# Two-layer transformer block, eight batches: the layer-A maxima moved one group of heads earlier, the V copies on two engines

## The reference, cut to what matters

```python
B, S, D = 8, 512, 128
def layer_A(x):                      # x is the normalised input
    Q = split_heads(x, 16)           # queries are x itself: 16 heads of width 8
    K = split_heads(x @ Wk + bk, 16)
    V = split_heads(x @ Wv + bv, 16)              # width 32
    attn = softmax(Q K^T + causal_mask)
    return x + gelu(attn @ V) @ Wf + bf
def layer_F(x):                      # 8 heads of width 64, 8 experts
    q, k = heads(x @ w_q), heads(x @ w_k)
    gates = sigmoid(x @ w_gate); sel = argmax(gates); gm = one_hot(sel) * gates
    values = einsum('bhne,ehdk,bnd->bhnk', gm, value_experts, x)
    out = softmax(causal(0.125 q k^T)) @ values
    return einsum('bhne,ehkd,bhnk->bhnd', gm, output_experts, out).sum(heads)
x = x + layer_A(layernorm(x)); x = x + layer_F(layernorm(x))
```

## Time and profile before

| | us |
|---|---|
| three runs, median (lowest to highest) | 1350.18 (1346.76 to 1360.11) |
| the profiled execution, own time | 1347.51 |
| its span, first to last instruction | 1345.8 |
| PE busy in the span | 1160.4 (86%) |
| ACT busy | 967.8 (72%) |
| DVE busy | 872.1 (65%) |

### The profile page before, as it was taken

The page is one execution under the profiler, slowest core; times in us unless marked ns, Lnnn a source line. Parts: engine busy times, 40 slices in busy tenths (PEclk is TensorE's granted clock), DMA queues, the critical chain, the costliest instruction groups (busy, mean ns, idle before and its releaser), DMA issues.

```text
span 1345.8 us, 19795 instructions
## 1 busy us (share of the span) xinstructions
PE 1160.4 (86%) x5720; PEld 634.3 (47%) x5720; DVE 872.1 (65%) x2725; ACT 967.8 (72%) x2671; POOL 306.1 (23%) x418
## 2 busy tenths in 40 slices
PE   2797898898888989899888989889898898989998
PEld 1126643366424754247433564336642475434653
DVE  4625757577574866758576585756758486764845
ACT  3894777948597686966779577795779767696660
POOL 1023311232102411133112231123220241112220
PEclk8567999999999999999999999999999999989999
DMA  6211240022300323003320124102240032300310
GB/s 184 65 66 33 51 123 20 4 64 67 109 2 4 80 79 81 2 11 72 105 55 2 45 50 112 37 4 64 59 114 4 4 80 77 83 2 3 72 48 24
DMA packets 43644, 72.71 MB, mean 54 GB/s; under 512 B 9664, under 2 KB 25408, under 8 KB 43216
## 3 DMA queue, kind: packets, MB, share of 16 engines
q1 hardware_dynamic: 38416, 54.67, 15.0%
q10 hardware_dynamic: 5120, 16.78, 4.8%
HBM read 45.34 MB, written 8.80 MB: 40 GB/s over the span
## 4 chain that ended last, share of the span: by engine, by line
PE 38%; ACT 27%; DVE 15%; issue 12%; DMA 5%; POOL 2%; SPq 2%; ACTq 0%; DVEq 0%; POOLq 0%
ACT masked L838 13%; ACT pt L895 9%; PE ps_m L624 7%; PE ps_o L615 6%; DVE masked L1153 4%; PE ps_exp L441 3%; PE ps_max L721 2%; DVE pt L1304 2%; PE ps_exp L531 2%; PE ps_m L441 2%; PE ps_exp L443 2%; DMA s2q<-mt_f 2%; PE ps_exp L442 2%; PE ps_m L443 2%; PE ps_m L442 2%
## 5 line engine op out<-in xcount | busy, mean ns | idle before, releaser
L1153 DVE CUSTOM_DVE_ANT_0 masked<-ps_max,mask 128x512 f32<-128x512 f32 (+3 forms) x768 | 353.5, 487 | 207.9 <-PE ps_max L529 100.0
L838 ACT ACTIVATE masked<-masked,low 128x512 f32<-128x512 f32 (+3 forms) x768 | 426.1, 558 | 65.5 <-DVE low L1153 62.2
L895 ACT ACTIVATE pt<-ps_exp 128x384 f32<-128x384 f32 (+1 forms) x480 | 247.7, 523 | 95.7 <-PE ps_exp L532 75.6
L1036 POOL TENSOR_SCALAR_AFFINE_SELECT pt<-pt 128x512 f32<-128x512 f32 (+2 forms) x192 | 133.3, 695 | 697.3 <-ACT pt L895 697.3
L624 PE MATMUL ps_m<-at,oe_sb 128*128 128x512 f32 x416 | 220.7, 620 | 5.6 <-DVE at L1204 3.5
L615 PE MATMUL ps_o<-pt,val 128*32 128x128 f32 (+6 forms) x1536 | 191.9, 476 | 12.1 <-POOL pt L1036 11.6
L529 PE MATMUL ps_max<-s2k,s1q 72*128 72x512 bf16 (+3 forms) x512 | 141.8, 326 | 34.4 <-DMA s2k<-onesb_d 21.9
L1204 DVE TENSOR_TENSOR at<-osb,hots 128x512 f32<-128x512 f32 x208 | 145.3, 705 | 15.5 <-PE ps_m L624 15.5
L838 ACT ACTIVATION_READ_ACCUMULATOR masked<-masked,low 128x1 f32 x768 | 149.7, 195 | 0.0
L529 PE MATMUL ps_exp<-s1q,s2k 75*128 75x384 bf16 (+3 forms) x384 | 104.9, 324 | 44.0 <-ACT pt L895 41.5
L531 PE MATMUL ps_exp<-s1q,s1k 128*128 128x256 f32 (+2 forms) x256 | 100.1, 402 | 19.9 <-DMA s2q<-mt_f 19.7
(11 more groups left out here) (170 smaller groups left out, 1919.0 us busy)
## 6 DMA issues: line engine op xcount, KB each, us to landing
hots<-hot_d ACTq DMA_DIRECT2D x64, 256.0 KB, 4.1
s1q<-parts_q SPq DMA_DIRECT2D x96, 96.0 KB
s2k<-parts_k SPq DMA_DIRECT2D x96, 96.0 KB
s1q<-pt SPq DMA_DIRECT2D x64, 128.0 KB, 2.3
s1k<-pt SPq DMA_DIRECT2D x64, 128.0 KB, 2.3
parts_q<-pt SPq DMA_DIRECT2D x24, 128.0 KB, 2.3
parts_k<-pt SPq DMA_DIRECT2D x24, 128.0 KB, 3.0
x_sb<-in_x SPq DMA_DIRECT2D x8, 256.0 KB, 2.8
```

The lines of the kernel that those rows point to most:

```text
L838: last = nc.scalar.activation(e, e, ACT.Exp, bias=low[:, g % 2, c:c + 1], scale=-1.0, accum_out=den[:, g % 2, c:c + 1])
L895: nc.scalar.activation(pt[:, (n % 2) * 4 + j, 0:c1 - c0], score_bank(k, u)[:, c0:c1], ACT.Exp).then_inc(exp_done[k].sem, 1)
L1036: nc.gpsimd.affine_select(out=v, in_=v, compare_op=ALU.is_ge, fill=0.0, base=0, pattern=[[0, HG[k]], [0, m], [1, P]], channel_multiplier=- ...
L1153: last = v.tensor_tensor_reduce(out=masked[:, u % JUNK, c0:c0 + w], in0=src[:, c0:c0 + w], in1=mask[:, S - w:S], scale=-1.0, scalar=POS, o ...
```

## The change

- `FIRST` has two max units beside each of F's units 12 to 23: group 0 at 12 to 17, group 1 at 18 to 23. `negate` and the transposition of group 0 move to F's units 21 (DVE) and 23 (PE).
- Pre holds group 2 (for the first batch, which has no F ahead of it, groups 0, 1 and 2).
- The 12 max units of group 3 stand beside A's units 2, 3, 5, 7, 9, 11, 13, 14, 16, 18, 20 and 22 (`LATE`).
- The keys' preparation moves two units later in F, to the units 3 to 6.
- ACT copies V's tiles 1 and 3, DVE tiles 0 and 2, with two semaphores `va` and `vb`.
- In `turn` one kept product comes ahead of the back projection, and one product each takes the next place.

```diff
-FIRST = {FIRST_AT + n: (n,) for n in range(STAGES * HG["A"])}
+A_UNITS = STAGES * HG["A"]
+FIRST = {FIRST_AT + n: (2 * n, 2 * n + 1) for n in range(A_UNITS)}
+LATE = {2 + 11 * n // 6: n for n in range(A_UNITS)}
+NEGATE_A, TRANSPOSE_A = 21, 23
+def pre_groups(a):
+    return (0, 1, 2) if a == 0 else (2,)
-PREP = {"q1": 0, "q2": 0, "K": 1, "k0": 1, "k_rest": 2, "k1": 3, "k2": 4}
+PREP = {"q1": 0, "q2": 0, "K": 3, "k0": 3, "k_rest": 4, "k1": 5, "k2": 6}
...
# PE, values_a and the first score units
-                    dst = free("A", "V", t, (va, a, t + 1))
+                    dst = free("A", "V", t, ((va, vb)[t % 2], a, t // 2 + 1))
-                    pe.wait_ge(va.sem, va.count(b, T))
+                    pe.wait_ge(va.sem, va.count(b, T // 2))
+                    pe.wait_ge(vb.sem, vb.count(b, T // 2))
# PE, attention_a
-                            if g + 2 < GROUPS:
-                                max_unit("A", a, g + 2, s * HG["A"] + j)
+                            if u in LATE:
+                                if LATE[u] == 0:
+                                    pe.wait_ge(restacked_a[3].sem, restacked_a[3].count(a, 16 * RESTACK["A"]))
+                                max_unit("A", a, 3, LATE[u])
# PE, attention_f
+                                for first in FIRST.get(u, ()):
+                                    g_a, m = divmod(first, A_UNITS)
+                                    if m == 0:
+                                        pe.wait_ge(restacked_a[g_a].sem, restacked_a[g_a].count(f + 1, 16 * RESTACK["A"]))
+                                    max_unit("A", f + 1, g_a, m)
+                                if u == TRANSPOSE_A:
+                                    maxima_transposed("A", f + 1, 0)
# PE, turn
+                if f >= 0:
+                    product(f, first + 1)
                 project_back(a, (0, 1, 2))
                 if f >= 0:
-                    product(f, first + 1)
+                    product(f, first + 2)
# ACT
+            def firsts(a, u):
+                for first in FIRST.get(u, ()):
+                    g, m = divmod(first, A_UNITS)
+                    denominators("A", a, g, m)
+                    if m == A_UNITS - 1:
+                        logs("A", a, g)
+            def values_a(a):
+                for t in range(1, T, 2):
+                    act.wait_ge(v_ready.sem, v_ready.count(a, t + 1))
+                    copy(val[:, t], ps_m[BANK[("A", "V", t)]][:]).then_inc(vb.sem, 1)
...
                 if k == "F":
                     sums(k, b, GROUPS - 1)
                     if b + 1 < B:
-                        for first in FIRST[NST * HG[k] - 1]:
-                            denominators("A", b + 1, 0, first)
-                        logs("A", b + 1, 0)
+                        firsts(b + 1, NST * HG[k] - 1)
+                        maxima("A", b + 1, 0)
# DVE
-                for t in range(T):
+                for t in range(0, T, 2):
                     dve.wait_ge(v_ready.sem, v_ready.count(a, t + 1))
                     v.tensor_copy(val[:, t], ps_m[BANK[("A", "V", t)]][:]).then_inc(va.sem, 1)
-                if a > 0:
-                    negate("A", a, 0)
+                                if u == NEGATE_A:
+                                    negate("A", f + 1, 0)
```

More of the change, by code:

```diff
@@ L263, in build @@
         parts_out = {n: sem(f"parts_out_{n}", 16 * PARTS) for n in "qk"}
[L264 removed]
+        v_ready, va, vb = sem("v_ready", T), sem("va", T // 2), sem("vb", T // 2)
         resid = sem("resid", 2)
@@ L642, in attention_a @@
                 n_units = STAGES * HG["A"]
-                for g in range(2):
-                    if g == 0 and a > 0:
-                        continue
+                for g in pre_groups(a):
                     pe.wait_ge(restacked_a[g].sem, restacked_a[g].count(a, 16 * RESTACK["A"]))
@@ L650, in attention_a @@
                             outputs(a - 1, "pre", n)
-                        if g == 1 and n == n_units // 2 - 1:
+                        if a == 0 and g == 1 and n == n_units // 2 - 1:
                             maxima_transposed("A", a, 0)
                 for g in range(GROUPS):
-                    if g + 2 < GROUPS:
-                        pe.wait_ge(restacked_a[g + 2].sem, restacked_a[g + 2].count(a, 16 * RESTACK["A"]))
                     pe.wait_ge(mrow["A"][g % 2].sem, mrow["A"][g % 2].count(a, 16 * MROWS["A"] * (g // 2 + 1)))
@@ L728, in turn @@
                 f, first = a - 1, T * E - TURN
+                if f >= 0:
+                    product(f, first + 1)
                 project_back(a, (0, 1, 2))
                 if f >= 0:
-                    product(f, first + 1)
+                    product(f, first + 2)
                 project_back(a, (3,))
                 if f >= 0:
-                    for u in range(first + 2, T * E - 2):
+                    for u in range(first + 3, T * E - 2):
                         product(f, u)
@@ L865, in attention @@
                 outs = b if k == "F" else b - 1
[L866 to L872, removed]
+                if k == "A":
+                    values_a(b)
+                for g in (0, 1) if k == "F" else pre_groups(b):
+                    for n in range(n_units):
+                        denominators(k, b, g, n)
+                        if g == 1 and n == (1 if k == "F" else n_units // 2 - 1):
+                            maxima(k, b, 0)
+                    logs(k, b, g)
                 if k == "F":
@@ L896, in attention @@
                                                  ACT.Exp).then_inc(exp_done[k].sem, 1)
-                            if m > 0 and g + 2 < GROUPS:
+                            if k == "A":
+                                if u - 1 in LATE:
+                                    denominators("A", b, 3, LATE[u - 1])
+                                    if LATE[u - 1] == A_UNITS - 1:
+                                        logs("A", b, 3)
+                            elif m > 0 and g + 2 < GROUPS:
                                 denominators(k, b, g + 2, m - 1)
@@ L902, in attention @@
                             if k == "F" and b + 1 < B:
-                                for first in FIRST.get(u - 1, ()):
-                                    denominators("A", b + 1, 0, first)
+                                firsts(b + 1, u - 1)
                             if s == 1 and j == 0 and g + 1 < GROUPS:
@@ L1233, in attention_a @@
                             u, m = (g * STAGES + s) * HG["A"] + j, s * HG["A"] + j
-                            if g + 2 < GROUPS:
-                                max_unit("A", a, g + 2, m)
+                            if u in LATE:
+                                max_unit("A", a, 3, LATE[u])
                             if a > 0 and ("A", u) in OUTPUTS:
@@ L1254, in attention_f @@
                                 for first in FIRST.get(u, ()):
-                                    max_unit("A", f + 1, 0, first)
+                                    max_unit("A", f + 1, *divmod(first, A_UNITS))
+                                if u == NEGATE_A:
+                                    negate("A", f + 1, 0)
                             if m == 1 and g + 1 < GROUPS:
```

2 lines of the change are left out of this document (removed).

## The result

The changed kernel takes 1382.91 us (median of five runs, 1377.35 to 1391.16) against 1350.18 (1346.76 to 1360.11): ratio 1.0226, 95% interval 1.019 to 1.0262. It is slower by 2.3%; 1335 us had been forecast, and 1360 was the upper end of the range.

What follows compares the result with a forecast made beforehand. Limits taken: PE in F's second half, DVE in pre, ACT in A's first half, PE in its second. Terms: -2.7 us a turn, seven turns -19, batch 0 +4: -15, so 1335 us; 8-in-10 range 1312 to 1360.

Steps and rivals of the forecast that it cites:

- The keys two units later: F's first half: later keys delay SP's transfers, so rows and group 0's keys land later; +0.9 us a turn.
- F's second half: F's units 12 to 23: 12 max units come, 22.3 us becomes 25.5; +3.2 us a turn.
- group 1's operand: F's unit 18: PE waits about 0.8 us for group 1's keys, half of it covered; +0.4 us a turn.
- rival 3: F's second half: ring of waits among PE, DVE, ACT, 2.5 us a unit with DVE's choices; total 1367 us; chance 0.12.
- Layer A: 12 max units leave its first half, 28.3 us becomes 22.3: -6.0 us a turn; second half -0.3.
- Between the layers: F's last exponential to pre's first max unit: `negate` now inside F, 7.0 us becomes 6.1; -0.9 a turn.
- The first batch: Batch 0: pre's 12 more units cost +8.8 us, the first half gains -4.9; +4 us once.
- The turn's kept product: Product moved ahead of the back projection fills PE's wait for the gelu; all moved products had cover: 0.
- Rival 2: Rows at unit 12 or group 1's keys at unit 18 cost 3 us more: 1352 us; chance 0.18.

Runs made afterwards that it cites:

- e2: Kernel before with only the keys' preparation moved to F's units 3 to 6: ratio 1.0268 to the kernel before, 1386.06 us.
- e3: Changed kernel with the keys' product and first copies back at unit 1, remainders and later copies left at units 4 to 6: ratio 1.0179, 1374.50 us.
- e4: Changed kernel with ACT's second pair of `hots` transfers issued at F's stage 6 instead of 5: ratio 1.0079, 1361.18 us.
- e1: Changed kernel with the keys' preparation back at F's units 1 to 4: ratio 0.9958 to the kernel before, 1343.63 us.
- e9: Changed kernel with keys back, second `hots` pair at F's stage 6, SP issuing keys ahead of F's rows for groups 0 and 1: ratio 0.9838, 1330.74 us.
- e6: Changed kernel with the keys back at units 1 to 4 and four `masked` buffers instead of three: ratio 0.9887, 1336.26 us.
- e8: Changed kernel with the keys back at units 1 to 4 and all four V copies on DVE: ratio 0.9938, 1344.16 us.
- e5: Changed kernel with the keys back at units 1 to 4 and ACT's second `hots` pair at F's stage 6: ratio 0.9896, 1335.00 us.
- e7: Kernel before with only ACT's second `hots` pair moved from F's stage 5 to 6: ratio 0.9962, 1348.30 us.
- e11: Kernel before with `hots` at F's stage 6 and SP issuing keys ahead of F's rows for groups 0 and 1: ratio 1.0046, 1357.89 us.

## Why the prediction was wrong

**The keys two units later: the step that failed.** It was sized at +0.9 us a turn and is +5.0 between F's unit 0 and unit 12 (e2 alone, which changes nothing else: +4.5 there, +5.4 for the turn). The mechanism was the one named: the issue of the rows is not delayed, their landing is, by what falls into the same stretch as `hots`. Its size was not. I took the bytes of the restack alone, 288 KB at 244 GB/s, 1.2 us; in the mean of seven turns the landing got 3.4 us longer (3.5 to 6.8) and the wait 3.5. Why the two together take so much longer than their bytes, no run shows. The base was wrong as well: I read the wait of 2.24 us off one turn, the longest of seven (0.6 to 2.2, mean 1.4), as I had taken the turns for equal at 160 to 160.3 us, where they take 158.4 to 161.0. All seven waits rose to between 4.6 and 5.5. The other part, 1.5 us ahead of unit 12, I had booked as a gain of 0.3. In the turn shown, unit 0's start to unit 3's score takes 6.5 us in both kernels: with the product at unit 1 PE waits 1.9 us for `xl`, and without it 0.95 for ACT's exponential and 0.89 for DVE's maximum. So the product was free at unit 1. At unit 3 it stands ahead of unit 4's score, at the lower clock (three passes of 0.63 us), while ACT waits. e3 shows that the product's place gives 0.8 us of these and the wait nothing; e4 that `hots` gives 2.6 us of the wait. The upper end of this step's range was +3, so that range did not hold either.

The rule of the Trainium skill, "DMA: Bandwidth & Descriptors", section "Issuing engines are not separate DMA queues", that transfers of all issuing engines share the 16 engines, agrees with e4, in which ACT's transfers alone moved: the wait went from 4.9 to 2.3 us.

**F's second half: direction right, size too small.** +3.2, with +0.4 for group 1's operand, against 5.3 in e1 and 4.6 in e9, which has no pause ahead of it, and 6.4 in the changed kernel. The engines' busy times were right: ACT 23.8 against 24.8 reckoned, DVE 20.7 against 21.1. What failed is "I take 25.5": three engines at 92, 85 and 73% don't interlock to within 1 us of the floor. The ring of rival 3 was reckoned at 2.0 us a unit; measured is 2.3 to 2.4, with PE waiting for DVE's maximum as it said. Its buffers are not the reason (e6). Group 1's operand is not either: no wait on it shows in e1 or e9. Of e1's 5.3 the pairs are about 4, by the turns of equal clock, and the rest goes with a granted clock that is lower in more of e1's turns. In the changed kernel all seven turns have 0.81 to 0.83 over the half, and it is 1.2 us longer than in e1; e2 shows 1.3 us more than before, with no max unit moved. That the long pause is what brings the clock down for longer is likely from these two, and not shown by itself. After e1 I held that the clock explained the rest too, and e9 refutes that: with no pause, and 0.94 granted in six of seven turns, the half is 28.0.

**Layer A: right, with some help of the clock.** First half and second, from first exponential to back projection: -6.3 forecast, -6.2 in e1, -5.5 in the changed kernel. The price of ACT's sums, 0.73 us a unit, carries it. PE was to be the busier engine of the first half, and it isn't: 18.4 us busy against ACT's 19.8. I had counted on the stretch at the lower clock to stay, and in the turn shown it went (granted 0.94 before, 1.00 after). At full clock the piece takes 44.9 to 45.1 us in three turns of the kernel before and 39.4 in three of the changed one: -5.5. What e1 has beyond that is that fewer of its turns have the lower clock.

**Between the layers: half right.** -0.9 forecast, -0.5 measured. With V's copies on DVE it is -1.0 (e8), so the gain is that of `negate`, and the shared copies take 0.4 of it back, by the wait for ACT behind its four sums. That wait had been seen, and the sharing was not costed apart from it.

**The first batch: right.** Pre +8.6 (first exponential at 64.24 against 55.68; forecast +8.8), all in all +5.3 against +4. The start of the first F is a scattered figure, though: the changed kernel and the five others that share its list up to there (e1, e3, e4, e5, e9) reach it at 158.6 to 163.0 us, mean 161.4, and the kernel before, e2, e7 and e11 at 155.7 to 159.0, mean 157.4. That is +4.0. **The turn's kept product:** it has no experiment of its own; the stretch from the last max unit's last product to the back projection has 19.2 us against 19.7, so no cost shows.

In sum -2.7 was forecast; the two steps put too low make it 4.1 and 2.8 more, between the layers 0.4, layer A 0.8: +5.4. Rival 2 named the row transfer at unit 12 and put 3 us on it or on group 1's keys, on which no wait came; the step missed by 4.1. Rival 3 gave the right sign, but its ring alone doesn't make the kernel slower: e1 has it and is at 0.9958.

## What to carry to other kernels

A small transfer that an engine waits for must be looked at with everything in flight beside it, whoever issued it: moving a producer that nobody waits for can push hundreds of KB in front of it. Before moving an instruction out of a place where its engine would idle anyway, ask what fills that place afterwards. Where work goes from a stage with one full engine to one in which three are nearly full, the floor of the fullest is not the forecast: here the half took 28.0 to 28.7 us where ACT, reckoned as the fullest, had 24.8, 13 to 16% more.

## What the runs showed of the hardware

Rows of a few KB, from the end of their issue to the start of the unit that needs them, means over seven turns: at most 2.0 us with neither bulk transfer ahead of them (e5 and e7, where PE doesn't wait), 3.5 with `hots` ahead (before), 4.2 with the late restack ahead and `hots` behind (e4), 6.8 with both ahead (changed).

Behind the pause of 4.8 us PE ran at 0.50 of its clock for some 10 us, from 354.8 to 365.0, although it was busy for 9.9 of them; behind that of 2.2 us it was some 3.5, and I had reckoned with no change there. The length doesn't follow from the pause alone: in e5's turn at 342, with a wait of 1.4 us, it was about 7, and in two other turns of e5, with waits of 1.2 and 1.3 us, there was no such stretch in the half. What decides it, the runs don't settle.
